# Value products of two steps issued together in the three heavy groups of a steady turn

## What is computed

```
L0: x = x + proj(softmax(q k^T) v)         attention over channels, 8 heads of 32
L1: x = gamma * Wo(attention(Wa x)) + x    1 head over the 1024 pixels, q and k of 32, v of 128 channels
L2: x = x + proj(attention(groupnorm(x)))  8 heads of 32 over the 1024 pixels, with biases
L3: n = groupnorm(x); x = proj(attention(n)) + n   the same without q, k, v biases
attention over pixels: sim = q k^T / sqrt(32), 1024 x 1024 for each head; softmax over a row; times v
```

## Time and profile before

| | |
|---|---|
| median of 3 runs | 2930.0 us |
| profiled execution, its own time | 2932.83 us |
| its span, first to last instruction | 2931.0 us |
| mean granted TensorE clock | 0.984 of full speed |
| TensorE busy (modelled) | 95% |
| VectorE, ScalarE, GpSimd busy | 64%, 53%, 73% |
| one steady turn (of 6) | about 350 us |

### The profile page before, as it was taken

How to read it: one execution, slowest core, us unless ns; L and a number is a source line. 1 busy time by engine, 2 the same in 40 slices (tenths; PEclk the granted TensorE clock), 3 DMA queues, 4 the chain that set the end, 5 groups by cost and what they waited for, 6 DMA issues and landing times.

```text
span 2931.0 us, 35836 instructions
## 1 busy us (share of the span) xinstructions
PE 2788.5 (95%) x12912; PEld 1382.1 (47%) x12912; DVE 1865.3 (64%) x3341; ACT 1548.1 (53%) x2794; POOL 2153.3 (73%) x740
## 2 busy tenths in 40 slices
PE   6879999999999999999999999999999999999998
PEld 4444445544455444554545444454445544444442
DVE  1346766576756667566675676656775566767672
ACT  2215655446555556455564465644655446566554
POOL 3208777688867788687886878758887687887876
PEclk9979999999999999999999999999999999999999
DMA  2060344313434145232450334412343303433340
GB/s 81 24 92 7 60 74 60 48 24 46 89 45 55 24 51 93 33 51 48 53 92 13 45 60 67 66 27 31 60 74 60 52 19 46 74 46 46 46 60 16
DMA packets 74387, 150.85 MB, mean 51 GB/s; under 512 B 9121, under 2 KB 10657, under 8 KB 74210
## 3 DMA queue, kind: packets, MB, share of 16 engines
q1 hardware_dynamic: 74210, 148.56, 33.2%
HBM read 20.46 MB, written 16.78 MB: 13 GB/s over the span
## 4 chain that ended last, share of the span: by engine, by line
PE 73%; ACT 9%; DMA 6%; DVE 5%; POOL 4%; issue 2%; SPq 0%; ACTq 0%; POOLq 0%; DVEq 0%
PE psum L1333 17%; PE psum L1358 13%; PE psum L1302 11%; PE psum L1241 6%; PE psum L1272 5%; ACT prob L943 5%; PE psum L1249 4%; PE psum L1354 4%; DMA K<-hi 3%; PE psum L1381 2%; DVE maxpart L1080 2%; PE psum L1176 2%; DMA Q<-max_rows 2%; POOL vT L839 2%; POOL acc L839 1%
## 5 line engine op out<-in xcount | busy, mean ns | idle before, releaser
L1080 DVE TENSOR_REDUCE maxpart<-psum 128x1 f32<-128x512 f32 x2176 | 1409.5, 684 | 737.3 <-PE psum L1302 712.9
L943 ACT ACTIVATE prob<-psum 128x512 f32<-128x512 f32 x2176 | 1222.1, 596 | 926.1 <-PE psum L1333 891.8
L839 POOL TENSOR_TENSOR acc<-acc,prob 128x2048 f32<-128x2048 f32 (+1 forms) x317 | 1129.9, 3564 | 164.2 <-ACT prob L943 134.7
L1333 PE MATMUL psum<-Q,K 104*128 104x512 f32 x2048 | 1082.7, 530 | 59.6 <-ACT prob L943 36.2
L1302 PE MATMUL psum<-K,Q 96*128 96x512 f32 x2048 | 828.1, 407 | 20.4 <-DVE maxpart L1080 14.1
L1333 PEld LDWEIGHTS psum<-Q,K 104*128 104x128 f32 x2048 | 385.5, 189 | 761.5 <-ACT prob L943 459.8
L839 POOL TENSOR_TENSOR vT<-vT,prob 128x2048 f32<-128x2048 f32 x122 | 556.2, 4559 | 22.0 <-ACT prob L943 11.6
L1358 PE MATMUL psum<-prob,vT 128*32 128x512 f32 x4096 | 559.5, 607 | 0.0
L1302 PEld LDWEIGHTS psum<-K,Q 96*128 96x128 f32 x2048 | 393.7, 192 | 160.0 <-issue 77.6
L839 POOL TENSOR_TENSOR acc<-prob 128x2048 f32<-128x2048 f32 (+1 forms) x58 | 212.1, 3657 | 326.2 <-ACT prob L943 173.1
L1358 PEld LDWEIGHTS psum<-prob,vT 128*32 128x32 f32 x4096 | 98.7, 108 | 193.0 <-ACT prob L943 107.5
(11 more groups left out here) (138 smaller groups left out, 2069.3 us busy)
## 6 DMA issues: line engine op xcount, KB each, us to landing
Q<-hi SPq DMA_DIRECT2D x128, 256.0 KB
K<-hi SPq DMA_DIRECT2D x128, 256.0 KB
Q<-lo SPq DMA_DIRECT2D x64, 256.0 KB
K<-lo SPq DMA_DIRECT2D x64, 256.0 KB
scratch<-xa SPq DMA_DIRECT2D x8, 1024.0 KB, 4.0
xb<-scratch SPq DMA_DIRECT2D x8, 1024.0 KB, 4.9
xa<-in_x SPq DMA_DIRECT2D x7, 1024.0 KB, 8.5
out<-hb SPq DMA_DIRECT2D x7, 1024.0 KB, 5.7
```

The source lines that it names most:

```text
L839: pool.tensor_tensor(total, first if a == 1 else total, this, ALU.add).then_inc(added, 1)
L943: act.activation(prob[STEP_STARTS.slot(b, start)][:, j, :], score_bank[(SCORES.rank[b.n][e] - 1) % SCORE_BANKS], ACT.Exp, scale=1.0 if lay ...
L1080: dve.tensor_reduce(maxpart[layer][:, a // NQ, a % NQ:a % NQ + 1], bank, AX_X, ALU.max).then_inc(max_free, 1)
L1333: pe.matmul(score_bank[(r - 1) % SCORE_BANKS], left, right, start=True, stop=True).then_inc(score_full, 1)
```

## The change

In groups (2,2), (2,3) and (3,0) of turns 3 to 8 the value sets stand only at the end of every even step (slots 3, 11, 19, 27). Each time TensorE issues two sets, of the step before last and of the last one; at slot 3 of (2,2) it is one set, at slot 3 of (2,3), (3,0) and (1,0) it is the last two of the group before. A `finish` in these groups waits for a slot with values, so that of the group before moves from slot 7 to slot 11; `invert` and `scale` are now counted from the `finish` and move from slots 9 and 12 to 13 and 16. The output pieces of layer 2 in (3,0) move from slots 16 to 30 to slots 20 to 30. All events are the same in number and kind; turns 0 to 2 and 9 have the same order as before.

```
 LAG = HPT
+PAIRED = {(2, 2), (2, 3), (3, 0)}
...
-              + [(3, 0, paced(0, 4, late3) + spread(SCALED, end, out2),
+              + [(3, 0, paced(0, 4, late3) + spread(SCALED + 4, end + 1, out2),
...
             plan.append(("evacuate",) + x[1:3])
-            pending.extend((clock + after, (kind,) + x[1:3]) for kind, after in
-                           (("finish", FINISH_AFTER), ("invert", INVERT_AFTER), ("scale", SCALE_AFTER)))
+            pending.append((clock + FINISH_AFTER, ("finish",) + x[1:3]))
+
+    def finished(of, now):
+
+        for kind, after in (("invert", INVERT_AFTER), ("scale", SCALE_AFTER)):
+            pending.append((now + after - FINISH_AFTER, (kind,) + of))
+        pending.sort(key=lambda x: x[0])
...
+                paired = groups is turns[3] and (layer, g) in PAIRED
+                with_values = j == HPT - 1 and (s % 2 == 0 or not paired)
...
-                while pending and pending[0][0] <= clock:
+                while pending and pending[0][0] <= clock and (with_values or pending[0][1][0] != "finish"):
                     x = pending.pop(0)[1]
                     (turning if x[0] == "finish" else plan).append(x)
+                    if x[0] == "finish":
+                        finished(x[1:], clock)
...
-                while j == HPT - 1 and len(late) > LAG:
+                while with_values and len(late) > LAG:
                     advance(plan)
```

More of the change, by code:

```diff
@@ L262, in advance @@
             plan.append(("evacuate",) + x[1:3])
-            pending.extend((clock + after, (kind,) + x[1:3]) for kind, after in
-                           (("finish", FINISH_AFTER), ("invert", INVERT_AFTER), ("scale", SCALE_AFTER)))
+            pending.append((clock + FINISH_AFTER, ("finish",) + x[1:3]))
[3 more added lines that the diff above has]
+        pending.sort(key=lambda x: x[0])
     turns = group_sequence()
-    for groups in turns:
+    for n, groups in enumerate(turns):
         plan = []
@@ L271, in plans @@
                 while late:
-                    advance(plan)
-                plan += [x for _, x in pending] + flat(pieces if ("max", 2, 0, 0) in pieces else cut(pieces))
-                pending.clear()
+                    if late[0][0] == "value" and late[0][3:] == (0, 0):
+                        while pending:
+                            x = pending.pop(0)[1]
+                            plan.append(x)
+                            if x[0] == "finish":
+                                finished(x[1:], clock)
+                    advance(plan)
+                while pending:
+                    x = pending.pop(0)[1]
+                    plan.append(x)
+                    if x[0] == "finish":
+                        finished(x[1:], clock)
+                plan += flat(pieces if ("max", 2, 0, 0) in pieces else cut(pieces))
                 if at + 1 < len(groups) and groups[at + 1][0] == 1:
```

## The result

The changed kernel took 2971.1 us (median of 4 runs, 2967.33 to 2978.67) against 2929.07 for the kernel before: a ratio of 1.0151, 95% interval 1.0136 to 1.0166. It is slower, as forecast, but by 42 us where 17 were forecast, and it lies above the range. The profiled execution took 2967.33 us, with a span of 2965.5 and a mean granted clock of 0.973 (before 0.984).

A forecast was written before the change was run, and what follows sets the result against it. TensorE, busy 95%, was taken to bind only between places where it waits. Per turn 2.3 - 2.5 + 3.7 = +3.5 us in turns 5 to 7, +2.3 in 3, 4, 8: +17.4, so 2947 us, range 2926 to 2964.

The forecast's parts named there:

- What two sets together save: Paired groups: a set moved behind another saves 0.34 us where TensorE sets the end; otherwise the move costs 0.86.
- a merger would have returned nothing: Rival from the span model: the six moves a turn counted at 0.34 give 0; 2959 us, chance 0.04.
- (2,2): Group (2,2): +2.3 us a turn, including 1.55 for a bank wait and 0.86 for moving set 6.
- The wait for the side bank: Slot 13 of (2,2): the row piece waits until `invert`'s first transpose has read the bank of `finish`; +1.55 us.
- (3,0) and (1,0): `finish` of (3,0) waits for GpSimd's adds queued behind a later `scale`: +3.7 us in turns 5 to 7, +2.5 in 3, 4, 8.
- (2,3): the step that failed: Group (2,3): TensorE sets the pace; three mergers, a hidden wait and set 6 gone from slot 31 give -2.5 us.
- The rival on the clock: TensorE runs at 1.2 GHz for one step after each of two waits a turn: +30 us, 2977 us, chance 0.03.
- the two new waits: TensorE waits for the bank at slot 13 of (2,2), 1.55 us, and for GpSimd at the `finish` of (3,0), 1 to 2.
- The walk: Step-by-step sum over (2,2), (2,3), (3,0) and the start of (1,0) in six steady turns: +17.4 us.
- Starvation behind doubled blocks: Rival: ScalarE and VectorE don't catch up behind nine doubled blocks a turn, 0.5 us each; some 2970 us, chance 0.08.
- the two new waits would not appear: Rival: bank free at slot 13 of (2,2), GpSimd done before TensorE in (3,0); 2931 us, no change, chance 0.22.
- every merger pays: Rival: neither side bank nor GpSimd holds TensorE, all 12 moves a turn save 0.34 us; 2902 us, chance 0.13.

The follow-up runs named there:

- the first two experiments: Changed kernel with set 6 of (2,2) left at slot 31: 2946.52 us; changed kernel with six needless products at that slot instead: 2951.94 us.
- the last pair on set 6: Kernel before with only set 6 of (2,2) moved to slot 3 of (2,3): 2949.66 us; same plus six needless products at slot 31: 2930.02 us.
- the needless products: Changed kernel with one maximum product at slot 31 of (2,2) issued six more times in each steady turn: 2951.94 us, ratio 1.0082.

## Why the prediction was right in direction and wrong in size

**What two sets together save.** Right. In (2,3) alone the steps at full clock save 2.38 us a turn (52.17 to 49.79); the prediction had 2.5 for the group itself. The 0.86 for a second set is seen by itself too: 0.85 a turn between the first two experiments, 0.87 in the last pair on set 6. By the span model of the Trainium skill, in Part 3 of TensorE: Matmul & The Clock Gate, which the prediction cites as a rival, a merger would have returned nothing; here the measurement decides. Another page of the Trainium skill, TensorEngine Tiling (Array Packing), says under Key Properties that changing the tiling mode drains TensorE. The rows are in line with that, though they don't single it out: a lone set costs 1.20 us between full scores, the one behind another set 0.86.

**(2,2).** Right: +1.6 in turn 5 for +1.44 forecast. The wait for the side bank was 1.41 us for 1.55, and it went with an earlier `invert`. In turn 7 the group was 52.8, with a stretch at the lower clock in it.

**(3,0) and (1,0).** Right in mechanism, and nearly in size: 20.5 us for 18.6. `invert` starts 19.10 us after the first score and `scale` at 20.98 (forecast about 20.7), the last add ends at 50.3 (forecast 50.1 on that scale, 1315.5 less the first score's 1265.4), and `finish` comes at 50.4 to 50.5 in turns 4 to 7, right behind it. In turns 3 and 8, with 6.8 us at the lower clock in the group, TensorE was last and `finish` came at 51.1; that clock is no part of the forecast. TensorE was ahead of GpSimd by 2.09 us in turn 5, where 1.7 were forecast, and by 0.35 to 0.37 in turns 4, 6 and 7.

**(2,3): the step that failed.** The prediction says of set 6: "Set 6 was free there. Moved to slot 3 of (2,3) it costs 0.86", and of the clock: "It is granted at full, 1.00, in all three windows with stalls of 0.5 to 0.9 us in them", with a chance of 0.03. The set was free in its slot only as long as one counts TensorE's time. It also kept TensorE at work between the scores and a wait that it couldn't shorten. Without it the idle place grew from 0.60 to 1.59 us, and within 2 us of that wait the clock went to 1.2 GHz in all six turns, in four of them for 10.2 to 13.7 us, in turns 3 and 8 for 3.4. That this was the cause, and not the set's own price or the waits at slot 13, is shown by the pair of kernels that differ from before by the one set: +24 us, and +4 with needless work in its place (medians beside the kernel before).

The rival on the clock was priced at 2977 us and had the place wrong: it was to come from the two new waits, for two steps a turn. That its price is near the 2971 measured is luck. Of the 78.5 us more at the lower clock, 56 lie in (2,3), behind a third one, which the prediction counted in its sum for (2,2) without asking how long TensorE now waits there. In time they cost 23.6 us, 327.6 against 304.0 with the needless products. Another 20 lie in (3,0), where they cost little: in turns 4, 6 and 7 they only shorten the wait for GpSimd, and in turns 3 and 8 `finish` comes 0.7 us later. The walk itself was not far off. With the needless products the change is at +24 us by the ratio (1.0082), where the walk had +17.4; its groups give +12.3, -9.1 and +20.5 for +8.6, -9.8 and +18.6. The 3.7 over in (2,2) lies in turns 3, 6 and 8, which are 53.9, 52.5 and 51.9 us long where the others are 51.0 to 51.1; their mean granted clock is 0.94, 0.97 and 0.97, that of the one in turn 5 is 1.00. In turns 3 and 6 the stretch at the lower clock begins 1 to 2 us behind the wait at slot 13, the place where the prediction's rival had put it. In turn 8 it begins 2.8 us into the group, ahead of that wait, as it does in turn 8 of the kernel before.

**The other rivals.** Starvation behind doubled blocks did not show: (2,3), with four of them, fell by what the sets save wherever its clock was full. That the two new waits would not appear was wrong: both did. That every merger pays came true in (2,3) alone.

**Left open.** Why the same wait brings the clock down for 10.2 to 13.7 us in some turns and hardly or not at all in others: turns 3 and 8 of the changed kernel have (2,3) at 52.1, the four between at 55.1 to 56.3. The length of a wait doesn't decide it alone. In the kernel before, TensorE waits 1.85 us at slot 16 of (3,0) in turns 3 and 8 and 1.61 in turn 4; the clock fell behind it in turn 8, and in turns 3 and 4 it stayed at full. Turn 3, the wait and the 20 us around and behind it:

```profile
582.59 0.50 PE L1333 MATMUL psum<-Q,K 104*128 104x512 f32 x1 [1.85 <-ACT prob L943]
...
579.40:600.00 20.60, 18.75 (x86) 9.02 (x84) 13.79 (x28) 9.93 (x18) 18.53 (x5) 1.00 0.59 70
```

## What to carry to other kernels

Work that costs nothing because TensorE would wait anyway may be what holds the clock: before moving it, add up how long TensorE is idle around the place without it, and price the case that the next 10 to 15 us run at the lower level. When a reordering costs more than its waits add up to, put needless products into the new waits, one at a time: if the time falls, it was the clock. The longest need not be the one; here it was that of the `finish`, 2.09 us, and the costly one had 1.59. And test a change that covers several groups one group at a time; here one of three gave 15 us, and the other two buried it.

## What the runs showed of the hardware

At an idle place of 1.59 us the clock fell from 2.4 to 1.2 GHz, and it stayed there for 13.7 us with TensorE busy for 13.52 of them (changed kernel, turn 5). Idle places of 1.61 and 1.85 us elsewhere, in turns 4 and 3 of the kernel before, left it at 2.4. The Trainium skill's page TensorE: Matmul & The Clock Gate, in "Why this matters for your kernels", asks for idle gaps between bursts to be short, as the clock falls otherwise. This trace agrees, but the gap that the page still allows is longer than 1.59 us; here the measurement decides. In the changed kernel such stretches add up to 95.6 us of the steady turns, in the kernel before to 17.1, and in the one with pairs in (2,3) and (3,3) to 3.4.

Six needless products, 1.54 us of work in a turn, made a kernel faster by 20 us (2949.66 to 2930.02), as they cost nothing in a wait that was there and kept the clock.
